# Queries and keys of a first attention: strips by DMA through DRAM, tokens normalised on ScalarE

## The reference, cut to what matters

```python
h = _ln(x, ln1_g, ln1_b)
qkv = h @ w_qkv + b_qkv
q, k, v = jnp.split(qkv, 3, axis=-1)
scores = jnp.einsum('bnihd,bnjhd->bnhij', qb, kc) * scale      # causal mask, then softmax
ob = jnp.einsum('bnhij,bnjhd->bnihd', attn, vc).reshape(B, T, C)
x = x + ob @ w_out + b_out
h2 = _ln(x, ln2_g, ln2_b)
m = jax.nn.gelu(h2 @ w1 + b1, approximate=False) @ w2 + b2     # the dense part, after the attention
```

## Time and profile before

| | us |
|---|---|
| median of 3 runs | 1021.27 (1019.35 to 1025.33) |
| the profiled execution | 1019.0 |
| its span in the trace | 1017.3 |
| first attention | from the start to about 236 |

### The profile page before, as it was taken

The page is one execution under the profiler, slowest core; times in us unless marked ns, Lnnn a source line. Parts: engine busy times, 40 slices in busy tenths (PEclk is TensorE's granted clock), DMA queues, the critical chain, the costliest instruction groups (busy, mean ns, idle before and its releaser), DMA issues. The chain is left out here.

```text
span 1017.3 us, 29043 instructions
## 1 busy us (share of the span) xinstructions
PE 926.0 (91%) x10222; PEld 593.8 (58%) x10222; DVE 815.7 (80%) x2276; ACT 783.2 (77%) x1546; POOL 434.1 (43%) x613
## 2 busy tenths in 40 slices
PE   5999999978999999999999999778888875899995
PEld 3788888854554444444444444455656554788862
DVE  4888888854877999688889899768888867888845
ACT  3889999978998888888888788367767634788844
POOL 3667777772452000000100001124688767666653
PEclk9999999997999999999999999899999956999998
DMA  8433333101000000222222222011111102323228
GB/s 255 170 132 131 129 132 127 45 19 33 1 2 1 1 1 1 76 81 78 63 73 92 74 73 63 1 56 40 37 54 55 44 28 82 85 82 82 81 59 215
DMA packets 61004, 72.60 MB, mean 71 GB/s; under 512 B 8874, under 2 KB 37804, under 8 KB 60864
## 3 DMA queue, kind: packets, MB, share of 16 engines
q1 hardware_dynamic: 50080, 59.36, 18.8%
q0 software_dynamic: 4544, 8.60, 2.6%
q10 hardware_dynamic: 6240, 2.79, 1.1%
HBM read 40.14 MB, written 31.49 MB: 70 GB/s over the span
## 5 line engine op out<-in xcount | busy, mean ns | idle before, releaser
L922 ACT ACTIVATE d__hf<-keep__banks,dense__d 128x512 f32<-128x512 f32 x288 | 185.8, 681 | 48.3 <-PE keep__banks L1160 47.3
L986 DVE TENSOR_TENSOR d__hl<-d__hf,d__hh 128x1024 f16<-128x1024 f32 x144 | 174.1, 1220 | 28.3 <-ACT d__hh L927 26.0
L906 POOL TENSOR_SCALAR d__rstd<-d__mv 128x4 f32<-128x4 f32 x16 | 14.2, 887 | 336.6 <-DVE d__mv L1114 336.6
L927 ACT ACTIVATE d__hh<-d__hf 128x1024 f16<-128x1024 f32 x144 | 152.2, 1057 | 4.6
L1158 PE MATMUL keep__banks<-dense__xh,dense__w1h 128*128 128x512 f16 x288 | 109.9, 382 | 3.0 <-ACT d__hf L922 1.7
L1158 PE MATMUL keep__banks<-d__hh,dense__w2h 128*128 128x512 f16 x288 | 109.2, 379 | 2.4 <-DVE d__tmp L1043 2.4
L1160 PE MATMUL keep__banks<-dense__xh,dense__w1l 128*128 128x512 f16 x288 | 109.9, 381 | 0.0
L1159 PE MATMUL keep__banks<-dense__xl,dense__w1h 128*128 128x512 f16 x288 | 109.9, 381 | 0.0
L1159 PE MATMUL keep__banks<-d__hl,dense__w2h 128*128 128x512 f16 x288 | 109.2, 379 | 0.0
L1160 PE MATMUL keep__banks<-d__hh,dense__w2l 128*128 128x512 f16 x288 | 109.2, 379 | 0.0
L390 POOL TENSOR_SCALAR_AFFINE_SELECT a__pt<-a__pt 128x512 f32<-128x512 f32 x128 | 83.9, 679 | 52.7 <-ACT a__pt L438 52.4
(11 more groups left out here) (356 smaller groups left out, 2433.6 us busy)
## 6 DMA issues: line engine op xcount, KB each, us to landing
rows<-a__blank SPq DMA_DIRECT2D x72, 268.0 KB, 3.2
d__G<-gates SPq DMA_DIRECT2D x64, 256.0 KB, 3.1
c__xin<-rows SPq DMA_DIRECT2D x39, 134.0 KB, 2.2
dense__stage<-e_w SPq DMA_DIRECT2D x16, 256.0 KB, 3.3
b__stage<-e_w SPq DMA_DIRECT2D x32, 128.0 KB, 2.3
c__yb<-parts SPq DMA_DIRECT2D x8, 256.0 KB, 8.2
c__yb<-parts ACTq DMA_DIRECT2D x8, 256.0 KB, 8.9
out<-c__xo SPq DMA_DIRECT2D x8, 256.0 KB, 2.3
```

Source lines behind the costliest of these rows:

```text
L922: act.activation(hf[:, q, f], HB[:, f], gelu, scale=1.0 / WS, bias=b1[:, at:at + 1]).then_inc(s_["h_free"], 1)
L927: act.activation(hh[:, j % (LEAD + 1), f - 1:f + 1], hf[:, q, f - 1:f + 1], ACT.Copy).then_inc(s_["hi_done"], 1)
L986: dve.tensor_tensor(hl[:, p, f], hf[:, q, f], hh[:, p, f], ALU.subtract).then_inc(s_["lo%d_done" % i], 1)
```

## The change

Queries and keys are no longer spread by TensorE. As soon as `high` and `low` exist, SyncE writes them to a DRAM tensor `heads` of six planes (three transfers of 128 KB, `high` twice), waits until they have landed, and fetches them back (three transfers of 128 KB) into `kq`, one tile that holds `ks` and `qs` in their strips; every piece is one row of 256 f16 numbers, 512 bytes. Scores wait for `landed`. The parts proj are gone, and with them the `spread` constant (512 KB) and ScalarE's copies; the rows of ones are written once at the start. `lift`, `vproj`, `qk` and `low` stand in quarter 1, `qk` in front of the exponentials of that quarter. The first norm is applied by ScalarE (new part hnorm, quarter 4, behind the exponentials and ahead of norm2 and split); GpSimd makes the -mean/std of both norms in one pair of instructions; VectorE's statistics of x move to quarter 1 (xstats). On SyncE the transfers of a block stand ahead of its five blanks, and the load of the later tokens and of the dense weights stands behind those of block 0.

```diff
 PARTS_0 = [
-    [("scores", 2, 0), ("vproj", 2, 0), ("shift", 3, 1), ("lift", 1, 0), ("weights", 3, 0), ("values", 4, 3),
-     ("copy", 4, 1)],
-    [("scores", 2, 1), ("mpad", 2, 0), ("qk", 1, 0), ("low", 1, 0), ("output", 5, 0), ("back", 4, 1),
+    [("scores", 2, 0), ("lift", 1, 0), ("vproj", 2, 0), ("shift", 3, 1), ("qk", 1, 0), ("xstats", 0, 0), ("low", 1, 0),
+     ("weights", 3, 0), ("values", 4, 3), ("copy", 4, 1)],
+    [("scores", 2, 1), ("mpad", 2, 0), ("output", 5, 0), ("back", 4, 1),
      ("weights", 3, 1), ("values", 3, 0), ("halves2", 6, 0), ("wlow", 0, 0)],
-    [("scores", 2, 2), ("proj", 1, 0), ("proj", 1, 1), ("shift", 2, 0), ("stats", 0, 0),
+    [("scores", 2, 2), ("shift", 2, 0), ("stats", 0, 0),
      ("weights", 3, 2), ("power", 0, 0), ("values", 3, 1), ("copy", 3, 0)],
-    [("scores", 2, 3), ("mpad", 2, 1), ("proj", 1, 2), ("proj", 1, 3), ("back", 3, 0), ("norm", 0, 0),
-     ("weights", 3, 3), ("values", 3, 2), ("norm2", 5, 0), ("split", 0, 0)]]
+    [("scores", 2, 3), ("mpad", 2, 1), ("back", 3, 0), ("norm", 0, 0),
+     ("weights", 3, 3), ("hnorm", 0, 0), ("values", 3, 2), ("norm2", 5, 0), ("split", 0, 0)]]
...
             sp.dma_start(x[:, 4:12, :], d["x"][:, 4:12, :]).then_inc(x_mid, 16)
...
+            for n in range(NB):
+                planes = heads[n % 2]
+                sp.wait_ge(high_done, n + 1)
+                wait(sp, landed[n % 2], 48 * (n // 2))
+                for i in (1, 3):
+                    sp.dma_start(planes[i:i + 2].rearrange("s p t -> p s t"), high[:]).then_inc(high_out, 16)
+                sp.wait_ge(low_done, n + 1)
+                sp.dma_start(planes[0:6:5].rearrange("s p t -> p s t"), low[:]).then_inc(low_out, 16)
+
+                sp.wait_ge(high_out, 32 * (n + 1))
+                wait(sp, st_full, n * 8 - 16)
+                for c, pair in enumerate((planes[2:4], planes[0:2], planes[4:6])):
+                    if c == 1:
+                        sp.wait_ge(low_out, 16 * (n + 1))
+                    sp.dma_start(kq[n % 3][c:P:4, :, :, BK:BK + TB].rearrange("r s a t -> r (s a) t"),
+                                 pair.rearrange("s (a r) t -> r (s a) t", a=4)).then_inc(landed[n % 2], 16)
+                if n == 0:
+                    sp.dma_start(x[:, 12:NT, :], d["x"][:, 12:NT, :]).then_inc(x_rest, 16)
+                    keep["fetch_dense"](sp)
+                    sp.wait_ge(blank_set, 1)
+                if n % 2 == 0 and n >= 4:
+                    sp.wait_ge(w_low, n - 2)
+                    keep["fetch_set"](sp, n // 2)
+                for i in range(5 * n, min(5 * n + 5, BLANKS * NC_)):
+                    sp.dma_start(blanks[:, i], blank[:]).then_inc(blanked, 16)
...
+                if what == "hnorm" and n < NB:
+
+                    wait(act, lift_full, n)
+                    act.wait_ge(shift_done, n + 1)
+                    for a in range(2):
+                        ins = act.activation(hn[:, a, :], x[:, 2 * n + a, :], ACT.Identity, scale=rstd[:, a:a + 1],
+                                             bias=shift[:, a:a + 1])
+                    ins.then_inc(hn_done, 1)
...
+                    pe.wait_ge(landed[n % 2], 48 * (n // 2 + 1))
```

More of the change, by code:

```diff
@@ L194, in parts_0 @@
                         step(what, s - 1, k)
-                elif what in ("stats", "power", "norm"):
+                elif what in ("xstats", "stats", "power", "norm", "hnorm"):
                     if s < AHEAD + 5:
@@ L231, in attention_0 @@
         rstd = m.sb("rstd", [P, 4])
-        shift2 = m.sb("shift2", [P, 2])
+        shift = m.sb("shift", [P, 4])
         hn2 = m.sb("hn2", [P, 2, C])
@@ L235, in attention_0 @@
         hn = m.sb("hn", [P, 2, C])
-        hT = m.sb("hT", [P, BK + TB])
+        hT = [m.sb(f"hT{p}", [P, BK + TB]) for p in range(2)]
         bv = m.sb("bv", [P, 4, P])
@@ L259, in attention_0 @@
         x_first, x_mid, x_rest = m.sem("x_first"), m.sem("x_mid"), m.sem("x_rest")
-        gate_in, spread_in = m.sem("gate_in"), m.sem("spread_in")
+        gate_in, unit_in, ones_in = m.sem("gate_in"), m.sem("unit_in"), m.sem("ones_in")
+        kq_clear = m.sem("kq_clear")
+        high_out, low_out = m.sem("high_out"), m.sem("low_out")
+        landed = [m.sem(f"landed{p}") for p in range(2)]
         xb_done = m.sem("xb_done")
@@ L326, in _ @@
             sp.dma_start(keep["gate0"][:], d["gate0"]).then_inc(gate_in, 16)
[L327 to L332, removed]
-                if i % 5 == 0:
-                    sp.wait_ge(hn_done, i // 5 + 1)
-                sp.dma_start(blanks[:, i], blank[:]).then_inc(blanked, 16)
+            for n in range(NB):
[22 more added lines that the diff above has]
+                    sp.dma_start(blanks[:, i], blank[:]).then_inc(blanked, 16)
@@ L345, in power @@
                 wait(pool, norm2_done, n - 5)
+                wait(pool, hn_done, min(n, NB))
                 settle(pool, passed_pool)
@@ L365, in step @@
                     power(n)
-                if what == "norm" and n >= 5:
+                if what == "norm":
+                    v = both_norms(n)
                     pool.wait_ge(rstd_done, n + 1)
-                    pool.tensor_scalar(shift2[:], mv[:, 2:4, 0], -1.0, 1.0, ALU.mult, ALU.mult).then_inc(shift2_own, 1)
-                    pool.wait_ge(shift2_own, n - 4)
-                    pool.tensor_tensor(shift2[:], shift2[:], rstd[:, 2:4], ALU.mult).then_inc(shift2_done, 1)
+                    pool.tensor_scalar(shift[:, v], mv[:, v, 0], -1.0, 1.0, ALU.mult, ALU.mult).then_inc(shift_own, 1)
+                    pool.wait_ge(shift_own, n + 1)
+                    pool.tensor_tensor(shift[:, v], shift[:, v], rstd[:, v], ALU.mult).then_inc(shift_done, 1)
+                    if n == 0:
+                        clears()
                 if what == "halves2":
@@ L415, in step @@
                     act.wait_ge(qk_full, n + 1)
+                    wait(act, high_out, 32 * n)
+                    wait(act, low_out, 16 * n)
                     for a in range(2):
```

155 lines of the change are left out of this document (67 added, 88 removed).

## The result

| | median, us | against before | 95% interval |
|---|---|---|---|
| kernel before, 4 runs | 1021.18 | | |
| changed kernel, 4 runs | 1068.18 | 1.0458 | 1.0424 to 1.0491 |

The change makes the kernel 47.0 us slower; the forecast was 39 us. The profiled execution of the changed kernel took 1068.2 us, its span is 1066.5, 49.2 more than before. The attention ends, by the table load of ScalarE behind it, at 280.72 instead of 235.04: 45.7 of the 49.2 us arise inside it.

A forecast was written before the change was run, and what follows sets the result against it. The prediction took a closed 12.78 us loop through ScalarE, TensorE and GpSimd as the bound. Its terms, 32 (eleven turns) + 2 (steps 3 to 5) + 5 (start) = 39 us, gave 1060 us, range 1050 to 1070.

The forecast's parts named there:

- What bounds the kernel: Steady steps: a closed loop through ScalarE, TensorE and GpSimd, 12.78 us a step, sets the time, not TensorE's work.
- What is removed, at nothing: Steady steps: TensorE's 1.7 us, ScalarE's 2.35 us and VectorE's two normalisations lie outside the loop, costed at nothing.
- hnorm, +0.78 a step: ScalarE's hnorm ahead of norm2 in the loop adds 0.78 us a step, bounds 0.7 to 0.88.
- qk ahead of the exponentials, +2.16 a step, bounds 1.9 to 2.3: Quarter 1: ScalarE waits for qk and makes `high` before exponentials and copy; qk to back grows from 1.53 to 3.69 us.
- The step, 15.7, bounds 15.4 to 16.0: Steady step after the change: 12.78 + 0.78 + 2.16 = 15.7 us.
- The eleven turns: Steps with halves2, hnorm and qk, from s = 6: 11 x 2.94 = 32 us, bounds 29 to 35.
- Rival B, the clock: Attention steps: TensorE, idle about 4.6 of 15.7 us, loses clock; +2 us a step, near 1085, fully 1105; chance 0.15.
- Rival C, the round trip: Steady steps: DRAM trip, forecast 6 us and hidden, is instead exposed; step grows 2 us, near 1085; chance 0.10.
- The start, +5 and +2: Block 1's transfers queue behind large loads on SyncE: +5 us, bounds 0 to 10; steps 3 to 5: +2.
- Steps 3 to 5: Early steps without halves2 and partly without norm2: +2 us for the three, bounds 0 to 4.
- the last steps, costed at nothing: Final steps of the attention, after the eleven turns: claimed unchanged.

The follow-up runs named there:

- experiment 4: Kernel before without the 8 matmuls a block that spread the low halves: 1019.98 us, ratio 0.9994.
- Experiments 8 to 11: Kernel before: wlow to quarter 1's end, 1024.99 us; also without half the spread matmuls, 1025.89; wlow to quarter 4, 1021.25; also without half the spread matmuls, 1015.37.
- experiments 10 and 11: Kernel before with GpSimd's wlow moved to quarter 4, behind norm2: 1021.25 us; the same without half of the spread matmuls: 1015.37 us.
- experiment 2: Changed kernel with the first norm back on VectorE, GpSimd still making both shifts: 1051.07 us, ratio 1.032.
- experiment 7: Kernel before with only the first norm moved from VectorE to ScalarE, ahead of norm2, GpSimd making both shifts: 1028.15 us, ratio 1.0074.
- experiment 5: Changed kernel with qk and low back in quarter 2, behind mpad and ahead of output, DMA trip kept: 1075.46 us, ratio 1.0528.
- experiment 6: Changed kernel with qk and low in quarter 2, blocks 1 to 15 fetching block 0's planes without waiting for their own writes: 1051.67 us, ratio 1.0325.
- experiment 1: Changed kernel with qk and low moved from ahead of quarter 1's exponentials to the end of quarter 1: 1084.28 us, ratio 1.0636.
- experiment 3: Changed kernel with the later tokens' load and the blanks behind block 1's transfers instead of block 0's: 1063.77 us, ratio 1.0431.
- experiment 8: Kernel before with only GpSimd's wlow (remainder of the dense weights) moved from quarter 2 to the end of quarter 1: 1024.99 us, ratio 1.0048.

## Why the prediction was right, and where it was off

- **What bounds the kernel.** The closed loop through ScalarE, TensorE and GpSimd, with TensorE's 25.00 of 25 us only seemingly full: shown by experiment 4 (no gain) and by the table of links. Experiments 8 to 11 show that it holds with little margin: other loops lie 0.2 to 0.3 us below, and then TensorE's matmuls count (5.9 us for eight a block, experiments 10 and 11).
- **What is removed, at nothing.** Right, by experiment 4 for half of TensorE's part. That ScalarE's copies were worth nothing in the loop wasn't tried alone; the table of links, which has no place for them, speaks for it.
- **hnorm, +0.78 a step.** Measured 0.83 in the changed kernel (experiment 2) and 0.68 in the one before (experiment 7, where TensorE's link came out 0.14 shorter).
- **qk ahead of the exponentials, +2.16 a step, bounds 1.9 to 2.3.** Over-sized. The link from qk to back gave 3.53 - 1.53 = 2.00, inside the bounds; but the link in front of it, costed as unchanged, gave 0.25 back, so the two together are (3.53 + 0.05) - (1.53 + 0.30) = 1.75. The 0.30 from lift to qk, read from before, was not a semaphore's cost but TensorE still at its earlier work; TensorE is idle now and starts qk 0.05 us after the copy's end. Experiment 5 shows 1.32, since in its order qk is itself 0.4 us late behind TensorE's work of quarter 1 (experiment 6).
- **The step, 15.7, bounds 15.4 to 16.0.** Mean 15.69, but of two errors that cancel, which is luck: 15.30 at full clock, below the lower bound, and 0.4 from the clock, which the sum didn't have. The eleven turns took 171.85 us (78.04 to 249.89, where norm2 comes first again) where they took 140.89: +30.96, forecast 32.
- **Rival B, the clock.** It came true in part. The granted clock is 0.93 in the mean, steps with slow windows take 15.8 to 16.1. The price was 0.4 us a step in the mean, not the 2 of the rival, since only part of what TensorE does is on the path: vproj between lift and qk (1.92 against 1.06 us), or qk itself (2.00 against 1.17 us to `high`). What makes the clock fall stays open. Experiment 2 shows that it goes with hnorm: with hnorm gone and lift waiting 1.1 us at most instead of 1.9, the clock stays at 1.00, with TensorE busy for 82% of the time against 81%. In experiment 6, where lift waits up to 1.9 us again, it is 0.95. But the wait alone doesn't decide it: in that kernel lift waited 1.88 us before 147.16 and before 178.08, and the vproj behind it still took 1.06 us. Nor need it be lift that waits: in experiment 1, at 0.78, a wait of TensorE of 1.77 us before 94.35 is for VectorE's `ob`. The Trainium skill, page "TensorE: Matmul & The Clock Gate", section "Why this matters for your kernels", says that it is the gaps between bursts that bring the clock down; the trace agrees in that longer gaps went with 0.93 and shorter ones with 1.00. The gaps that the page warns of are longer than any here (1.89 us at most from 75 to 225 us), and the clock fell all the same; the measurement decides.
- **Rival C, the round trip.** It was to take 6 us and be hidden with 2 to spare. It took 6.6 to 8.9 in the steady steps of the changed kernel (`high` ready at 130.53, the last of the three fetches issued at 134.8, landed 2.6 later: 6.9) and 7.0 to 9.6 in experiment 5. The three issues of a fetch hold SyncE for 1.9 us, the first transfer of the fetch is not issued before both writes have landed, and blanks and dense weights share the 16 DMA engines. The cover held, with nearly nothing to spare: the scores of steady steps wait 1.3 us or less, four times.
- **The start, +5 and +2.** The mis-sized term: it took 14.0 us. Block 1 came at +9.0 (bounds 0 to 10) instead of +5. SyncE was free for its transfers at 25.90, near the forecast 26.5, and held the first write for 1.5 us only (24.43 to 25.90). From there the forecast left 5.5 us to a landing near 32; it took 10.2, to 36.1. The prediction said that the transfers queue behind the bytes, but its sum gave this no time: a write of `high` took 5.4 us to land instead of 1.9 (experiment 3), in a stretch where the 16 DMA engines move 348 GB/s (20 to 30 us), and the fetch waits for that landing. By experiment 3 the loads in front cost 5.2 of the 9.0; the other 3.8, a later `high` and a trip longer than the spreading that it replaces, are there without them. Steps 3 to 5 took 5.0 us more (14.0 - 9.0) instead of 2 (bounds 0 to 4). The rows of the changed kernel's windows there:

```profile
30.00:40.00 10.00, 4.01 (x34) 3.59 (x34) 3.46 (x7) 0.56 (x1) 0.00 (x0) 0.51 0.68 229
40.00:50.00 10.00, 8.17 (x244) 5.39 (x243) 8.16 (x22) 6.19 (x13) 6.92 (x13) 1.00 0.46 145
```

In the window with the wait of 5.99 us for block 1 the clock is at 0.51, that is nearly all of it at 1.2 GHz, and it is back at 1.00 in the next. It had begun to fall before that wait: the window from 20 to 30 us has 0.81. How much of the 3 us too many is the clock and how much the loop of these steps wasn't told apart.
- **Behind the attention.** The span grows by another 3.5 us that no edit touches: 1.9 between 682 and 903 us and 1.6 in the last stretch. The medians differ by 47.0, so 2.2 of it is that the profiled execution of before took that much less than its median, and that of the changed kernel did not. The rest stays open.

In sum: 32 became 31.0 and 2 + 5 became 14.0; the last steps, costed at nothing, took 0.7 more (45.7 - 31.0 - 14.0), and the kernel behind the attention 1.3 by the medians (47.0 - 45.7). 39 became 47, nearly all of the difference at the start. Without the 0.4 us a step of the clock it would have been about 43, still in the forecast's own range.

## What to carry to other kernels

When an engine looks full, follow one instruction that recurs in each step back through queues and semaphores until it closes on itself; if the durations add up to the step, only work on that loop has a price, and work removed elsewhere, even from the fullest engine, has none, as long as that loop stays the longest (here others were 0.2 to 0.3 us behind). A step moved in an in-order queue must be followed in every engine that has a share of it (experiment 1 was lost in VectorE's), and a trip that is hidden in steady steps is paid by the first blocks, where little runs beside it, and more so behind large loads: where transfers queue behind others, the time until those have landed belongs in the sum. Work put into the loop has a second price when TensorE's clock falls with it.

## What the runs showed of the hardware

- VectorE's smallest instructions are stretched by GpSimd: L537 (128x16, two inputs in SBUF) takes 0.23 us alone and 1.11 us beside GpSimd's 128x512 tensor_tensor of 1.16 us. Its group, from the lines of the kernel before and then of experiment 8, up to 240 us:

```profile
L537 DVE TENSOR_TENSOR a__mpad<-a__mx,a__mpad 128x16 f16<-128x16 f32 x32 | 7.8, 245 | 1.1
```

```profile
L537 DVE TENSOR_TENSOR a__mpad<-a__mx,a__mpad 128x16 f16<-128x16 f32 x32 | 14.8, 463 | 1.1
```

245 ns in the mean before, 463 with wlow moved. The Trainium skill, page "GPSIMD Engine Reference", section "8. Key points", says that GpSimd shares its SBUF interfaces with VectorE, with contention for instructions of VectorE that have two SBUF inputs; the trace agrees, and shows that a short one can last nearly as long as the whole GpSimd instruction. The copy in front of it (L536, 128x16, one input in SBUF) was stretched too: 1.17 us in experiment 8 (149.43) where it takes 0.20 alone.
- TensorE's clock fell in a stretch where it was busy for 81% of the time and was full in another with 82%. In the changed kernel vproj took 1.91 us behind a wait of 1.89 us (94.36) and 1.06 us behind one of 0.96 (110.25); in experiment 6 it took 1.06 us behind one of 1.88 (178.08).
- A trip of queries and keys through DRAM, 128 KB at a time in pieces of 512 bytes, took 2.2 us (a write) and 2.9 us (a fetch) from issue to landing, in the median. As a whole it took 6.3 us at the start once the large loads were out of its way, and 6.6 to 9.6 us in steady steps. SyncE's six issues are 3.3 us of that in experiment 5 (0.89 + 0.50 + 1.91, from 121.45) and 4.2 in the step of 109.22 of the changed kernel (1.78 + 0.47 + 1.90).
